# The node network moved into the first turns of a scatter loop, and node rows kept in rank order

## The reference

```python
# layer 2: h is the edge network's output, col the destination of each edge
agg = summed / jnp.maximum(counts, 1.0)[:, None]
z = jnp.concatenate([x, agg], axis=1)
z = jax.nn.relu(z @ w2a + b2a)
x = _layernorm(x + (z @ w2b + b2b))
# layer 3
deg = jax.ops.segment_sum(ones, hs, n)            # hs = src: out-degree
sqrt_d_inv = deg ** (-0.5)
scaled = sqrt_d_inv[:, None] * feats_n
agg = jax.ops.segment_sum(scaled[ts], hs, n)      # ts = dst
msg = sqrt_d_inv[:, None] * agg
x = _layernorm(x + jax.nn.relu(msg @ weight.T))
```

## Time and profile before

| | us |
|---|---|
| runs | 10054.02, 10061.37, 10061.08 |
| median | 10061.08 |
| profiled execution, own time | 10058.45 |
| profiled execution, span of its trace | 10056.7 |

### The profile page before, as it was taken

How to read it: one execution, slowest core, us unless ns; L and a number is a source line. 1 busy time by engine, 2 the same in 40 slices (tenths; PEclk the granted TensorE clock), 3 DMA queues, 4 the chain that set the end, 5 groups by cost and what they waited for, 6 DMA issues and landing times. The chain is left out here.

```text
span 10056.7 us, 82805 instructions
## 1 busy us (share of the span) xinstructions
PE 4611.3 (46%) x14536; PEld 2828.8 (28%) x14536; DVE 5050.1 (50%) x11741; ACT 1627.6 (16%) x3231; POOL 5827.1 (58%) x5427
## 2 busy tenths in 40 slices
PE   6277677633333332222222223666666666444443
PEld 5122223222222221212211222333333333333332
DVE  6277777765555544444444454344444443333333
ACT  1322222221111211111211111111111112000002
POOL 2456556535656555555455564465555644888885
PEclk8588888865555555555555555678777886555555
DMA  2422223442323233333233332344444441444445
GB/s 67 125 54 56 52 56 58 53 104 80 87 79 90 82 78 83 85 86 86 74 84 89 84 89 69 109 134 126 128 128 128 131 88 23 36 36 36 36 36 100
DMA packets 681407, 811.12 MB, mean 81 GB/s; under 512 B 312002, under 2 KB 519285, under 8 KB 680182
## 3 DMA queue, kind: packets, MB, share of 16 engines
q0 software_dynamic: 317424, 531.92, 26.0%
q1 hardware_dynamic: 321574, 120.52, 4.6%
q10 hardware_dynamic: 42336, 157.90, 4.4%
HBM read 581.27 MB, written 228.61 MB: 81 GB/s over the span
## 5 line engine op out<-in xcount | busy, mean ns | idle before, releaser
L1774 POOL DMA_INDIRECT big<-table_layer,slot_rows_L x2400 | 2326.1, 969 | 1686.9 <-issue 1148.5
L2437 POOL DMA_INDIRECT sums_by_source<-msg,to x800 | 1252.4, 1566 | 260.4 <-issue 208.6
L1793 PE MATMUL own_ps_L<-of_tile_L,big 50*128 50x16 f32 x1224 | 283.7, 369 | 2435.0 <-DVE fade_L L1891 1531.0
L983 POOL DMA_INDIRECT big<-table_layer,idx_L x912 | 958.6, 1051 | 662.7 <-DVE h L1160 333.9
L2072 PE MATMUL ps<-big,w 128*128 128x512 f32 x1792 | 935.7, 671 | 254.4 <-ACT big L2091 159.2
L2041 POOL DMA_INDIRECT big<-table_layer,rec_m x904 | 878.4, 972 | 275.4 <-issue 269.0
L2130 DVE SCALAR_TENSOR_TENSOR big<-ps,nbb,big 128x128 f32 x1792 | 545.7, 346 | 924.3 <-remote 613.7
L1793 PEld LDWEIGHTS own_ps_L<-of_tile_L,big 50*128 50x128 f32 x1224 | 272.4, 324 | 2510.9 <-issue 2496.2
L1074 PE MATMUL sums_L<-h,ident 128*128 128x512 f32 x1344 | 715.1, 682 | 361.7 <-DVE h L1160 191.0
L1785 PE MATMUL psH_L<-w,h 128*128 128x256 f32 x1584 | 674.6, 606 | 387.7 <-ACT big L1838 307.1
L1913 DVE TENSOR_TENSOR_SCAN big<-h,products_L 128x1122 f32<-128x1122 f32 x300 | 747.5, 2492 | 25.4 <-issue 1.0
(11 more groups left out here) (443 smaller groups left out, 7465.7 us busy)
## 6 DMA issues: line engine op xcount, KB each, us to landing
hidden_edge_parts<-big ACTq DMA_DIRECT2D x72, 768.0 KB
hidden_edge_parts<-big ACTq DMA_DIRECT2D x72, 640.0 KB
big<-table_layer,slot_rows_L POOLq DMA_INDIRECT x2400
h<-in_edges ACTq DMA_DIRECT2D x75, 384.0 KB
h<-in_edges ACTq DMA_DIRECT2D x75, 320.0 KB
table_layer<-xr SPq DMA_DIRECT2D x49, 298.0 KB
big<-table_layer,idx_L POOLq DMA_INDIRECT x912
big<-table_layer,rec_m POOLq DMA_INDIRECT x904
```

Source lines behind the costliest of these rows:

```text
L983: G.indirect_dma_start(out=g[b][:, u, s, :], out_offset=None, in_=table, in_offset=bass.IndirectOffsetOnAxis(ap=at, axis=0)).then_inc(gath ...
L1774: G.indirect_dma_start(out=ring[b][:, s, :], out_offset=None, in_=tab1_d[l], in_offset=bass.IndirectOffsetOnAxis(ap=at_rows[b][:, s, R_POS ...
L1793: last = PE.matmul(own_ps[:, c * SLOTS:(c + 1) * SLOTS], own1T[:, c * P:(c + 1) * P], of_tile[b % 2][:, :], start=True, stop=True)
L2437: G.indirect_dma_start(out=sum_d[s], out_offset=bass.IndirectOffsetOnAxis(ap=to[u][:, s:s + 1], axis=0), in_=msg[u][:, s, :], in_offset=No ...
```

## The change

The node network's own stage is gone. Its work stands in the scatter stage: tile 0, then tiles 1 to 4, before the loop, and the other 44 tiles in the first 11 turns, four in each, by code in the engines' programs between the items (a second loop without it runs the other turns). Its buffers are single now. Turn i works on the tiles that turns from i + 1 on may need. TensorE begins each early turn only when the group of the turn before is normalised. x stays on chip; the sums lie in rank order in DRAM (the sources of an item are `R_POS`, an integer, in place of `R_SUM`), so the last layer reads x from `xr`. It works in nine groups of 2, 3, 4, 6, 6, 7, 7, 7 and 7 tiles, and GpSimd stores the 49 tiles of the result by indirect transfers. The out-degrees used at the end are the ones in rank order. Core of the diff:

```diff
-                    for j in range(NT):
-                        pool.wait_ge(norm_ok, j + 1)
-                        G.indirect_dma_start(out=x3_d, ..., in_=xr[:, j, :], in_offset=None).then_inc(x_out, 16)
+                TB, ROUNDS = 4, (NT - 5) // 4
+                def later(i):
+                    return i + 2, ds(i * TB + 5, TB), lambda j: ds(i * TB + 5 + j, 1), TB
+                def both_loops(eng, n, turn):
+                    with eng.Fori(0, ROUNDS) as i:
+                        turn(i, True)
+                    with eng.Fori(ROUNDS, n) as i:
+                        turn(i, False)
 # SP, at the end of an early turn
+                            sp.wait_ge(lin, q * 2)
+                            degree_rows(q, tiles, n, 0)
 # TensorE
+                    def turn(i, early):
+                        if early:
+                            q, tiles, tile, n = later(i)
+                            pe.wait_ge(norm_ok, q)
+                        for u in range(U):
+                            item(i, u)
+                            if early and u == 0:
+                                turn_rows(q, n)
+                            if early and u in (2, 3):
+                                hidden(q, tiles, n, u - 2, 0, q)
+                            if early and u == 5:
+                                output(q, n)
 # ScalarE
+                            item(i, u)
+                            if early and u == 1:
+                                store(q, n)
+                            if early and u in (3, 4):
+                                relu(q, n, u - 3)
+                            if early and u == 6:
+                                square_root(q, n)
+                            if early and u == 7:
+                                normalise(q, tile, n)
 # VectorE
+                            item(i, u)
+                            if early and u == 0:
+                                fetch(q, tiles, n)
+                            if early and u == 6:
+                                join(q, tiles, n)
+                            if early and u == 7:
+                                finish(q, tiles, n)
 # VectorE, in an item
-                            srcs = rec[u][:, :, R_SUM].bitcast(fp32)
+                        V.tensor_copy(srcs[v][:, :], rec[u][:, :, R_POS])
+                        dve.drain()
 # VectorE, join
+                        dve.wait_ge(fin, q + 1)
+                        dve.wait_ge(norm_ok, q)
+                        V.tensor_tensor(scaled[:, 0:n, :], psO[...], bc(inv[:, tiles], 2, D), ALU.mult).then_inc(read, 1)
+                        V.tensor_tensor(xg[:, 0:n, :], xr[:, tiles, :], bc(b5[:, :], 1, n), ALU.add)
+                        dve.drain()
+                        V.tensor_tensor(xg[:, 0:n, :], xg[:, 0:n, :], scaled[:, 0:n, :], ALU.add)
 # last layer
-                            sp.dma_start(xn[:, :, :], rows(x3_d, 0, NT)).then_inc(xn_in, 16)
-                            sp.dma_start(rows(out, a, z), xn[:, a:z, :]).then_inc(out_out, 16)
+            for size in (2, 3, 4, 6, 6, 7, 7, 7, 7):
+                for j in range(NT):
+                    lanes = min(P, N - j * P)
+                    pool.wait_ge(norm_ok, j + 1)
+                    G.indirect_dma_start(out=out, out_offset=..., in_=xr[0:lanes, j, :], in_offset=None
+                        ).then_inc(out_out, 16)
```

More of the change, by code:

```diff
@@ L2178, in _ @@
[L2178 to L2208, removed]
-                            last = V.scalar_tensor_tensor(xr[:, j, :], psO[i % 2][:, (j - a) * P:(j - a + 1) * P],
-                                                          inv[:, j:j + 1], xr[:, j, :], ALU.mult, ALU.add)
-                        last.then_inc(read, 1)
-                        dve.drain()
-                        moments(dve, a, z).then_inc(var_ok, 1)
-                        if i:
-                            finish(i - 1)
-                    finish(len(GB) - 1)
@@ new lines, in _ @@
+                    for w in range(2):
+                        q, tiles, tile, n = first(w)
+                        turn_rows(q, n)
+                        for f in range(2):
+                            hidden(q, tiles, n, f, 1 - w, 1)
+                        output(q, n)
+                    n_turns = turns_of_slots(pe)
+                    pe.wait_ge(pad_ok, 1)
+                    with pe.Fori(0, ROUNDS) as i:
+                        turn(i, True)
+                    pe.wait_ge(norm_ok, ROUNDS + 2)
@@ new lines, in _ @@
+                    act.sem_inc(msg_ok, 2)
+                    act.wait_ge(iso_max, 1)
+                    A.activation(iso[:, :], iso[:, :], ACT.Sqrt).then_inc(iso_root, 1)
+                    for w in range(2):
+                        q, tiles, tile, n = first(w)
+                        store(q, n)
+                        for f in range(2):
+                            relu(q, n, f)
+                        square_root(q, n)
+                        normalise(q, tile, n)
+                    both_loops(act, turns_of_slots(act), turn)
@@ L2424, in _ @@
+                    dve.wait_ge(iso_root, 1)
+                    V.reciprocal(iso[:, :], iso[:, :])
+                    fetch(*first(1)[:2], TB)
+                    for w in range(2):
+                        q, tiles, tile, n = first(w)
+                        join(q, tiles, n)
+                        finish(q, tiles, n)
+                    both_loops(dve, turns_of_slots(dve), turn)
                 @block.gpsimd
                 def _(pool):
+                    G.memset(h[:, NT:NTP, :], 0.0).then_inc(pad_ok, 1)
@@ L2426, in _ @@
                     pool.sem_inc(passed, S * U)
+                    pool.wait_ge(pad_ok, 1)
+                    for s in range(S):
+                        pool.dma_start(sum_d[s][NT * P:NPAD, :], flat(h[:, NT:NTP, :])).then_inc(added[s], 16)
                     n = turns_of_slots(pool)
```

658 lines of the change are left out of this document (314 added, 344 removed).

## The result

The changed kernel takes 9929.74 us (median of 4 runs, 9862.87 to 9957.69) against 10061.23 of the kernel before (4 runs): ratio 0.985, 95% interval 0.982 to 0.989. Forecast were 9923 us, range 9860 to 9975. Two more chips gave 0.984 (0.981 to 0.988) and 0.975 (0.974 to 0.977).

A forecast was written before the change was run, and what follows sets the result against it. GpSimd's indirect adds, 1.870 us each, were taken to pace the scatter loop. Span 10056.7 - 201.5 + 54 + 9.3 = 9918.5 us; with offsets to execution time and median, 9923. Range 9860 to 9975, the forecast case's own 9895 to 9955.

The forecast's parts named there:

- Five tiles up front: Ahead of the scatter loop: five tiles in place of 49 bring the first add 201.5 us earlier, ends 197 and 206.
- The early turns: First 11 scatter turns: TensorE needs 64.8 us a turn against 59.8 for the adds; the loop grows by 54 us.
- all hidden: Rival for the early turns: TensorE's clock rises, a turn needs 58.2 us, all work hidden, total 9873 us; chance 0.21.
- The signs that I had named: Early turns: openings 65 us apart, adds in bursts, some 55 us of GpSimd idle time ended by ScalarE's message copy.
- first hidden half, less 0.4: Early turn, after item 2: 7.4 us at the slow clock, 0.4 covered by register loads, so 7.0.
- second hidden half: Early turn, after item 3: the other half of the hidden matmuls, taken as 5.8 us, between 3.8 and 7.4.
- output: Early turn, after item 5: the node network's output, 1.95 us fast, up to 3.6 slow, taken as 3.0.
- the rest (40.1 + 0.9 + 3.8 + 4.2): Early turn: TensorE's unhindered turn 40.1 us, transposes 0.9, delay behind VectorE's join 3.8, new wait for normalised rows 4.2.
- the wait at the turn's edge: Early turns: TensorE's next turn starts only once the group is normalised, which adds 4.2 us a turn.
- Adds land no later: Scatter loop: new row order does not lengthen landings; the opposing rival, 10123 us at 1 us longer, had chance 0.05.
- Two-input passes: Rival in the early turns: VectorE's three added two-SBUF-input passes stop GpSimd, 23 us more, total 9946 us; chance 0.03.
- The last layer: After the last add: x's load gone, 49 indirect stores added; 97 us from first load to end, cost 9.3 us.

The follow-up runs named there:

- the doubled half: Changed kernel with the hidden layer's half-matmuls of the first hidden half issued twice in the 11 early turns; 10008.0 us, ratio 0.992.
- the kernel with the network ahead: Changed kernel with all 13 node-network groups ahead of the scatter loop and none in it; 10123.99 us against 10006.49 of the kernel before.
- buffers kept: Changed kernel with the dropped on-chip tensor, its instruction and the earlier DRAM tensors declared again; 8366.66 us on the third chip, ratio 0.976.

## Why the prediction was right and where it was wrong

**The total** was right to 7 us by luck. By the profiled span the errors are +3.1 ahead of the loop, -47.8 in it, +7.8 behind it and +74.4 in the part that I had put at nothing, +37.5 in all; the median then lay 28 us under the profiled execution. The stages are what counts.

**Five tiles up front: right.** -198.4 against -201.5, inside 197 to 206. From the first scaling (8300.67) to the opening of turn 0 (8334.01) 33.3 us passed, where I had 30.5 (8225.94 to 8256.4). The small tile took the 8.1 that I gave it, the second group 25.2 in place of 22.4. The clock was 0.62, lower than the 0.74 that I started from.

**The early turns: the step that failed.** I took 64.8 us a turn, over the adds' 59.8, so that the loop would grow by 54 us; the turn was 57.6 to 58.5, the 58.2 of the rival "all hidden", and the loop grew by 6.2. The signs that I had named (turns 65 apart, some 55 us of GpSimd's idle time ended by message copies) did not come. By its terms, in turn 1:

| term, us | taken | measured |
|---|---|---|
| first hidden half, less 0.4 | 7.0 | 4.0 |
| second hidden half | 5.8 | 3.9 |
| output | 3.0 | 2.5 |
| the rest (40.1 + 0.9 + 3.8 + 4.2) | 49.0 | 47.5 |

The rival's 58.2 holds as a sum and not term by term: it had 3.4 + 3.8 + 2.0 for the first three rows, 1.2 too little, and 49.0 for the rest, 1.5 too much. The reading that misled me was the earlier trace rows: a half at the slow clock late in the node network, taken as what a mixed load gets, and as if the clock rose only late there. The windows of that stage show both levels in turn (before; granted clock before the last two numbers):

```profile
8369.50:8376.00 6.50, 3.65 (x20) 2.24 (x18) 2.57 (x14) 0.60 (x1) 0.00 (x0) 1.00 0.00 1
8376.50:8389.50 13.00, 12.22 (x17) 4.62 (x18) 1.32 (x3) 4.27 (x10) 3.88 (x4) 0.50 0.07 21
8390.00:8396.50 6.50, 3.48 (x20) 2.24 (x18) 2.66 (x15) 0.76 (x2) 0.00 (x0) 1.00 0.00 1
```

The group of the earlier trace rows fell into one slow stretch of a stage that had 0.78 up to 8437.5. In the early turns the second half always ran at 1.00, the first at 0.74 to 0.87. I had weighed the rival at .21 with the right row for it (0.74 over the whole stage against 0.51) and let one late group outweigh that. The term of the wait at the turn's edge was right (3.92 against 4.2), and so was the price of a turn that is too long, as the doubled half showed (73 us over the loop before, against 70 by the formula).

**Adds land no later: right.** GpSimd's idle times that end with the landing of an earlier add are 44.1 us in 145 times against 34.8 in 114, 0.3 each as before and as all others in the loop, and the loop of the kernel with the network ahead is 1493.1.

**Two-input passes: I read the rule against too few rows.** The loop's +6.2 us is GpSimd's busy time: 1259.1 against 1252.4; its idle time behind the first add is the same to 0.4 us. The add that I quoted (8479.86) had started 0.13 us before VectorE's product. An add that starts under one is another matter; timeline of the changed kernel, turn 5:

```profile
8624.76 1.55 POOL L2465 DMA_INDIRECT sums_by_source<-big,to  x1 [0.30 <-issue]
8625.73 0.69 DVE L2406 TENSOR_TENSOR big<-psR,source_rows 128x512 f32<-128x512 f32 x1 [5.75 <-PE psR L2265]
8626.51 0.69 DVE L2410 TENSOR_TENSOR big<-big,lower 128x512 f32<-128x512 f32 x1
8626.62 2.01 POOL L2465 DMA_INDIRECT sums_by_source<-big,to  x1 [0.30 <-issue]
...
8628.93 1.55 POOL L2465 DMA_INDIRECT sums_by_source<-big,to  x1 [0.30 <-issue]
```

The product of two SBUF tiles began at 8626.51, the add 0.11 later, and it took 2.01 instead of 1.55, as if it had begun shortly before the product's end at 8627.20. Over the loop 52 adds start inside such a product; the 29 of them that start 0.05 to 0.54 us after it have a mean of 1.85 (2.07 where they start 0.05 after it, 1.93 where 0.19), the others 1.55. Inside the comparison with PSUM 80 adds start and have 1.55. Before, 11 started in a product, with 1.65 in the mean. The Trainium skill (GPSIMD Engine Reference, 8. Key points) says that GpSimd contends with VectorE instructions in a 2-port perf mode or with two SBUF inputs. For two inputs these rows agree, for transfers issued under one, and a case of it stood in the trace before (an add at 8539.97 took 1.97, 0.14 us into a product).

Two inputs are not the only condition, and here I overlooked the larger share. VectorE's wide copy of the sources reads one SBUF tile, and adds that start under it are longer too; timeline of the kernel before:

```profile
8573.98 0.76 DVE L2404 COPY spread<-rec_s 128x512 f32<-128x512 f32 x2
8574.07 1.76 POOL L2437 DMA_INDIRECT sums_by_source<-msg,to  x1 [0.30 <-issue]
```

In the kernel before, 59 adds start in such a copy: the 44 that start 0.05 us or more after it have a mean of 1.75, the 15 earlier ones 1.55, and then the copy is the longer one (0.46 to 0.50 in place of 0.43). Over the loop the time above 1.55 an add sums to 11.6 us before, of which 8.6 stand under copies and 1.1 under products, and to 18.3 after, with 4.4 and 8.7; most of the rest after are 21 adds during which a copy starts 1.1 to 1.3 us in (1.70 in the mean). In which mode the copy ran no row shows. The growth of this time lies in the early turns: 14.3 against 5.6 us in the first eleven, 4.0 against 6.0 in the others. So the effect that the rival named is real, but its size was not the length of the three added passes (23 us): the adds that start under those are 1.6 us longer in all, and the rest of the 6.7 us comes from adds that now meet the products and copies of the scatter itself at other moments.

**The last layer: right in kind, too small.** From the first load to the end 106.7 us against 97 predicted. The first stores of the groups issued a little later (27.1, 33.8, 44.2, 53.9, 61.8 against 26, 32, 42, 50, 58 for the supply), so that the last issue ended at 99.6 and not at 94: +5.6. From its end to the end of the span 7.1 us passed where I allowed 3: +4.1. The interval from the last add to the first load is 1.9 shorter than before. That 3 had no row behind it. Part of the +5.6 is the contention of the paragraph above, which I had not put into this stage: eight of the 49 stores start under sums of two SBUF tiles on VectorE and take 1.37 to 1.86 us in place of 0.96, 5.9 us more in all; 2.5 of these fall on the last store that waited for rows and those after it.

```profile
9885.98 1.09 DVE L2541 TENSOR_TENSOR q<-q 128x896 f32<-128x896 f32 x1
9886.04 1.86 POOL L2519 DMA_INDIRECT out<-xr,nid  x1 [0.30 <-issue]
```

**The front that the change leaves alone: the term put at nothing.** "Nothing of weight before them", I wrote; it was +74.4 and +98.6 on two chips, and the cause stays open. On the chip without unexplained pauses the layer-0 loop of the changed kernel is as long as with buffers kept. Elsewhere four traces of kernels without these buffers have 1659 to 1662 us (first and second chip) and one has 1609 (fourth); six with one or more of them have 1560 to 1627 (first, second, fourth, fifth). So a difference of placement is possible, and it was not shown: on no chip with pauses did two kernels run that differ in the buffers alone. The sum of ScalarE's pauses does not carry it (744 us in loops of 1627 and of 1662), and on the second chip 64 of the 98.6 us lie outside this loop. Why the gain on the third chip is 210 us and not the 175 of the stages is open as well, since the kernel before left no trace there.

## What to carry to other kernels

Work moved under a bounding engine is free up to the slack of each turn and costs every microsecond behind it: read the slack from a turn in which nothing holds the moved-to engine back, and price the moved matmuls at both clocks, because the stage they land in has a clock of its own (here 0.71 in the early turns against 0.50 in the late ones). Split two traces by stage before comparing them: here a part that nobody touched moved by 74 us, more than the error of any step. A store by index has a price at the end of a kernel that a plain store has not (issue 1.26 us per 128 rows, and 8.65 us from the last issue until all is over, against 4.7 from the last rows with plain stores), so let it run out early. And look for wide VectorE passes (copies, and products or sums of two SBUF tiles) where GpSimd issues its transfers: here they made single issues up to 0.9 us longer.

## What was not expected of the hardware

- One program took 8359 us on one chip and 9930 and 9951 on two others (the kernel before 8570, 10006, 10016, 10061 and 10088). The loop bound by GpSimd's issue has the same length on all (1500.8 to 1502.8 in the changed kernel). The part of the changed kernel up to the last layer-2 add takes 6707 us on the fast chip and 8299 and 8325 on two others, and in its layer-0 loop only the traces of the slower chips have pauses in which engines wait for nothing shown; how much of the difference these carry was not shown.
- A copy of 128x512 integers to floats on VectorE costs what a float copy does: 447 and 444 ns.
- The granted clock can change inside a stretch of 58 us: 0.60, 0.94 and 0.69 in three parts of one turn.
